# Layer 1 of a four-layer graph network: mark matmuls first, an edge sum in one pass over high and low halves, row one-hots from a distance, their bf16 copy on GpSimd

## The reference, cut to what matters

```python
g_l = (h @ W_l.T).reshape(b, n, H, F)                  # H = 8 heads, F = 16
g_r = (h @ W_r.T).reshape(b, n, H, F)
g_sum = g_r[:, :, None, :, :] + g_l[:, None, :, :, :]  # every pair (i, j)
e = einsum('bijhf,f->bijh', leaky_relu(g_sum, 0.2), w_attn)
e = where(mask == 0, -inf, e * mask)
a = softmax(e, axis=2)
attn_res = einsum('bijh,bjhf->bihf', a, g_r)
out = leaky_relu(attn_res.reshape(b, n, H * F), 0.2)
x = layernorm(x + out)
```

## Time and profile before

| | us |
|---|---|
| median of 3 runs | 1573.96 |
| lowest and highest | 1572.91, 1576.82 |
| the profiled execution | 1573.45 |
| its span in the profile | 1571.7 |

### The profile page before, as it was taken

The page is one execution under the profiler, slowest core; times in us unless marked ns, Lnnn a source line. Parts: engine busy times, 40 slices in busy tenths (PEclk is TensorE's granted clock), DMA queues, the critical chain, the costliest instruction groups (busy, mean ns, idle before and its releaser), DMA issues. The chain is left out here.

```text
span 1571.7 us, 28366 instructions
## 1 busy us (share of the span) xinstructions
PE 1380.7 (88%) x9081; PEld 1163.2 (74%) x9081; DVE 1251.6 (80%) x2450; ACT 1044.8 (66%) x2743; POOL 55.9 (4%) x88
## 2 busy tenths in 40 slices
PE   3666588999999999999999986999999999995764
PEld 2555366688888888888888885888888888884654
DVE  4888478778787878878787644898889989987888
ACT  2565588766666666666666213888888888886554
POOL 1000000000000000000000000010010110100000
PEclk9998699999999999999999997999999999998877
DMA  2220266888887878878888665988787788771122
GB/s 75 68 67 27 112 258 247 320 310 292 299 304 291 308 288 308 306 283 309 299 296 303 236 243 206 349 274 279 271 271 280 267 275 278 268 253 47 45 74 67
DMA packets 137585, 367.61 MB, mean 234 GB/s; under 512 B 12896, under 2 KB 71904, under 8 KB 137440
## 3 DMA queue, kind: packets, MB, share of 16 engines
q1 hardware_dynamic: 137040, 365.81, 65.8%
q10 hardware_dynamic: 400, 0.00, 0.0%
HBM read 231.54 MB, written 134.22 MB: 233 GB/s over the span
## 5 line engine op out<-in xcount | busy, mean ns | idle before, releaser
L874 DVE TENSOR_TENSOR b_wt<-bank,b_aT 128x512 f32<-128x512 f32 (+1 forms) x192 | 109.7, 599 | 95.2 <-PE bank L688 88.1
L647 PE MATMUL wide<-b_vv,put_w 128*128 128x512 f32 (+1 forms) x384 | 170.9, 527 | 12.8 <-DVE b_vv L823 10.8
L1054 PE MATMUL wide<-W2c,c_h 128*128 128x128 f32 x1280 | 173.9, 275 | 0.0
L1054 PEld LDWEIGHTS wide<-W2c,c_h 128*128 128x128 f32 x1280 | 170.4, 193 | 3.3
L664 PE MATMUL bank<-b_wt,b_SITl 128*128 128x136 f32 x1280 | 160.1, 280 | 9.4 <-DVE b_wt L874 9.4
L664 PEld LDWEIGHTS bank<-b_wt,b_SITl 128*128 128x128 f32 x1280 | 156.3, 190 | 16.0 <-DVE b_wt L874 12.0
L823 DVE TENSOR_TENSOR b_vv<-duo,b_vv 128x512 f32<-128x512 f32 (+1 forms) x192 | 113.8, 600 | 51.4 <-ACT b_vv L744 51.4
L688 PE MATMUL bank<-b_grl,b_SJl 128*128 128x128 f32 x1280 | 153.4, 275 | 0.6 <-ACT b_aT L751 0.6
L688 PEld LDWEIGHTS bank<-b_grl,b_SJl 128*128 128x128 f32 x1280 | 148.7, 192 | 2.8 <-issue 2.6
L1184 DVE TENSOR_REDUCE c_var<-c_ysq 128x4 f32<-128x512 f32 (+1 forms) x192 | 113.5, 591 | 43.2 <-ACT c_ysq L1113 43.0
L648 PE MATMUL wide<-b_SI,put_m 128*128 128x512 f32 (+1 forms) x192 | 131.6, 686 | 0.0
(11 more groups left out here) (212 smaller groups left out, 3180.4 us busy)
## 6 DMA issues: line engine op xcount, KB each, us to landing
si_d<-b_SI SPq DMA_DIRECT2D x64, 640.0 KB, 2.9
sj_d<-b_SJ SPq DMA_DIRECT2D x64, 640.0 KB, 4.1
sit_d<-b_SIT SPq DMA_DIRECT2D x64, 640.0 KB, 5.3
b_SJl<-sj_d SPq DMA_DIRECT2D x64, 640.0 KB, 5.8
b_SITl<-sit_d SPq DMA_DIRECT2D x64, 640.0 KB, 5.9
c_SJ<-sj_d SPq DMA_DIRECT2D x64, 640.0 KB, 5.3
c_SI<-si_d SPq DMA_DIRECT2D x64, 640.0 KB, 6.6
c_SIT<-sit_d SPq DMA_DIRECT2D x64, 640.0 KB, 4.2
```

Of the source, the lines that this page charges most:

```text
L647: pe.matmul(out, e.put_w[:, pos, :], vv[:, (pos + k) % 2, 0:width(k)], start=(pos == 0), stop=False)
L874: v.tensor_tensor(wt[:, mb, 4 * k:4 * k + rr, 0:P].rearrange("p r (h f) -> p r h f", h=HEADS), ring[k][:, 0:P * rr].rearrange("p (r h f) - ...
L1054: d = pe.matmul(bY[k][:, a:a + P], h[:, k, a:a + P], e.W2c[:, :], start=False, stop=(j == last))
```

## The change

Four things change, all in layer 1:

- **Sum over halves.** ACT casts `wt` to fp32r into the first 136 columns of `wh` (three instructions, L816 after), DVE writes the rest, `wt` minus that, into the other 136 (three, L929), and PE sums both with 10 fp32r matmuls of 272 columns (L673), for 10 fp32 ones of 136. ACT copies two results out (`ol`, `os`; L776, L777), and DVE adds them once for four graphs (L897).
- **Marks first.** The three mark matmuls of a step stand together ahead of the first score (L659), and no longer one behind each score.
- **Row one-hots from a distance.** ACT takes the absolute distance of each slot number from the middle of a row's range in f32 (L360), and DVE compares it with half the row's length in one `tensor_scalar` (L369), for a `scalar_tensor_tensor` over two tensors.
- **The bf16 copy `SIb`** is made by GpSimd (L377), in a queue of its own.

```diff
 def start_rows(act, e, s, K, pos, late):
-    act.activation(s.after[:, :], e.number1[:, :], ACT.Relu, bias=e.unfirst[:, bass.ds(n, 1)]).then_inc(s.after_ok, 1)
+    act.activation(s.far[:, :], e.number1[:, :], ACT.Abs, bias=e.unmid[:, n:n + 1]).then_inc(s.far_ok, 1)
 def select_rows(v, e, s, K, pos, late):
-    v.scalar_tensor_tensor(s.SI[:, pos % 4, :], e.number1[:, :], e.end[:, bass.ds(n, 1)], s.after[:, :],
-                           ALU.is_le, ALU.min).then_inc(s.si_ok, 1)
+    v.tensor_scalar(s.SI[:, pos % 4, :], s.far[:, :], e.half[:, n:n + 1], None, ALU.is_le).then_inc(s.si_ok, 1)
+def shorten_rows(pool, s, n):
+    pool.wait_ge(s.si_ok, n + 1)
+    if n >= 1:
+        pool.wait_ge(s.s_mm, 3 * n)
+    pool.tensor_copy(s.SIb[:, :], s.SI[:, n % 4, :].bitcast(F32)).then_inc(s.sib_ok, 1)
...
@@ PE
-                        pe.matmul(out, e.put_w[:, pos, :], vv[:, (pos + k) % 2, 0:width(k)], start=(pos == 0), stop=False)
-                        pe.matmul(out, e.put_m[:, pos, :], s.SI[:, pos % 4, chunk(k)], start=False,
+                        pe.matmul(out, e.put_w[:, pos, :], vv[:, (pos + k) % 2, 0:width(k)], start=False,
                                   stop=(pos == R - 1)).then_inc(e_mm, 1)
+                    def mark_rows():
+                        if pos == 0 and n > 0:
+                            pe.wait_ge(es_ok, K)
+                        for k in range(CHUNKS):
+                            pe.matmul(bE[:, chunk(k)], e.put_m[:, pos, :], s.SI[:, pos % 4, chunk(k)], start=(pos == 0), stop=False)
...
-                        pe.wait_ge(w_ok, 3 * o + 3)
-                        pe.wait_ge(wa_ok, o + 1)
+                        pe.wait_ge(wl_ok, 3 * o + 3)
...
-                            d = pe.matmul(ring[1][:, 0:W], SITl[:, ob, j, :], wt[:, ob, j, :],
+                            d = pe.matmul(ring[1][:, 0:2 * W], SITl[:, ob, j, :], wh[:, ob, j, :],
@@ ACT
+                        act.copy(ol[:, (o // Q) % 2, o % Q, :], ring[1][:, W:2 * W])
                         act.copy(os[:, (o // Q) % 2, o % Q, :], ring[1][:, 0:W]).then_inc(os_ok, 1)
...
-                    if N:
-                        shorten_rows(act, s, K, pos + 1, inner or g >= 1)
...
+                    if S:
+                        for k in range(CHUNKS):
+                            js = slice(tiles(k).start, tiles(k).stop)
+                            act.wait_ge(w_ok, 3 * m + k + 1)
+                            act.wait_ge(wa_ok, m + 1)
+                            if m >= 2:
+                                act.wait_ge(o_mm, m - 1)
+                            act.copy(wh[:, mb, js, 0:W], wt[:, mb, js, :]).then_inc(wh_ok, 1)
@@ DVE
+                        f.add(v.tensor_tensor(part, part, ol[:, fours(n) % 2, :, :], ALU.add))
+                        f.wait()
...
+                    if S:
+                        for k in range(CHUNKS):
+                            js = slice(tiles(k).start, tiles(k).stop)
+                            v.wait_ge(wh_ok, 3 * m + k + 1)
+                            v.tensor_tensor(wh[:, mb, js, W:2 * W], wt[:, mb, js, :], wh[:, mb, js, 0:W].bitcast(F32),
+                                            ALU.subtract).then_inc(wl_ok, 1)
```

More of the change, by code:

```diff
@@ L296, in _ @@
                 q.add(v.tensor_copy(e.first[:, :], bank[:, 0:B]))
-                q.add(v.tensor_scalar(e.unfirst[:, :], bank[:, 0:B], -1.0, None, ALU.mult))
                 q.add(v.tensor_reduce(worst[:, 0:1], bank[:, P:P + B], AX.X, ALU.max))
@@ L300, in _ @@
                 q.wait()
-                q.add(v.tensor_tensor(e.end[:, :], e.first[:, :], e.deg[:, 0, :], ALU.add))
+                q.add(v.tensor_scalar(e.half[:, :], e.deg[:, 0, :], 0.5, -0.5, ALU.mult, ALU.add))
+                q.add(v.scalar_tensor_tensor(e.unmid[:, :], e.deg[:, 0, :], 0.5, e.first[:, :], ALU.mult, ALU.add))
                 q.add(v.tensor_scalar(worst[:, 0:1], worst[:, 0:1], float(ECAP), None, ALU.is_gt))
@@ L304, in _ @@
                 q.wait()
+                q.add(v.tensor_scalar(e.unmid[:, :], e.unmid[:, :], -1.0, -0.5, ALU.mult, ALU.add))
                 q.add(v.tensor_tensor(e.general[:, :], worst[:, 0:1], worst[:, 1:2], ALU.max))
@@ L358, in start_rows @@
         act.wait_ge(s.si_ok, n)
-    act.activation(s.after[:, :], e.number1[:, :], ACT.Relu, bias=e.unfirst[:, bass.ds(n, 1)]).then_inc(s.after_ok, 1)
+    act.activation(s.far[:, :], e.number1[:, :], ACT.Abs, bias=e.unmid[:, n:n + 1]).then_inc(s.far_ok, 1)
 def select_rows(v, e, s, K, pos, late):
     n = 8 * K + pos
-    v.wait_ge(s.after_ok, n + 1)
+    v.wait_ge(s.far_ok, n + 1)
     if late:
         v.wait_ge(s.u_mm, 3 * n - 9)
-    v.scalar_tensor_tensor(s.SI[:, pos % 4, :], e.number1[:, :], e.end[:, bass.ds(n, 1)], s.after[:, :],
-                           ALU.is_le, ALU.min).then_inc(s.si_ok, 1)
[L372 to L378, removed]
+    v.tensor_scalar(s.SI[:, pos % 4, :], s.far[:, :], e.half[:, n:n + 1], None, ALU.is_le).then_inc(s.si_ok, 1)
[4 more added lines that the diff above has]
+    pool.tensor_copy(s.SIb[:, :], s.SI[:, n % 4, :].bitcast(F32)).then_inc(s.sib_ok, 1)
 def split_low(v, s, bank, K, pos, late, hi_count):
@@ L466, in layer1_packed @@
         s.C = sb("C", [P, 2, P], F32R)
-        s.after = sb("after", [P, ECAP], BF16)
+        s.far = sb("far", [P, ECAP])
         s.SI = sb("SI", [P, 4, ECAP], F32R)
@@ L489, in layer1_packed @@
         wt = sb("wt", [P, 2, TILES, W])
+        wh = sb("wh", [P, 2, TILES, 2 * W], F32R)
         os = sb("os", [P, 2, Q, W])
+        ol = sb("ol", [P, 2, Q, W])
         rden = sb("rden", [P, Q, HEADS])
@@ L530, in layer1_packed @@
         wa_ok = sem("wa_ok")
+        wh_ok = sem("wh_ok")
+        wl_ok = sem("wl_ok")
         o_mm = sem("o_mm")
@@ L622, in _ @@
                 pool.memset(mark[:, ECAP:ECAP + 1], 0.0).then_inc(pad_ok, 1)
+                for n in range(B):
+                    shorten_rows(pool, s, n)
             @block.tensor
@@ L691, in step @@
                     if A and not T:
-                        if pos == 0 and n > 0:
-                            pe.wait_ge(es_ok, K)
+                        mark_rows()
                         score(0)
@@ L888, in step @@
                     if joined(n):
-                        f = Steps(v, seq_c, 5 * fours(n))
-                        f.n = 3
+                        f = Steps(v, seq_c, 6 * fours(n))
+                        f.n = 4
                         f.wait()
@@ L1900, in adjacency_stack @@
         first = sb("first", [P, B])
-        unfirst = sb("unfirst", [P, B])
-        end = sb("end", [P, B])
+        unmid = sb("unmid", [P, B])
+        half = sb("half", [P, B])
         general = sb("general", [P, 1], I32)
@@ L2072, in adjacency_stack @@
         e.first = first
-        e.unfirst = unfirst
+        e.unmid = unmid
         e.identb = identb
-        e.end = end
+        e.half = half
         e.general = general
```

19 lines of the change are left out of this document (10 added, 9 removed).

## The result

The changed kernel takes 1623.5 us (median of 4 runs, 1619.3 to 1627.0) where the kernel before took 1573.8 beside it: a ratio of 1.030, 95% interval 1.0286 to 1.0321. It is 3% slower. The forecast was 1617, in a range of 1555 to 1648. The total was nearly right by luck, for two of its terms were not right: the overlap's was 21 us too large, the drain's 28 us too small.

What follows compares the result with a forecast made beforehand. PE bounds the overlap, with DVE nearly as full; after the change DVE was followed as the limit. Overlap +26, fill -5 and drain +22 make +43 on 1573.45, about 1617 us; own range 1600 to 1635, over the cases 1555 to 1648.

Steps and rivals of the forecast that it cites:

- the overlap's: Overlapped stretch of layer 1: steps of 12.2 us on average, 0.55 more than before, times 48 steps: +26 us.
- the drain's: Drain of layer 1: steps of 7.0 us on average where they took 5.6, +19 us over 13 steps.
- POOL's hold: DVE in layer 1: POOL's bf16 copy holds up `C`, by 0 to 1.4 us, taken as 0.7 a step.
- Fill: Fill of layer 1: about 0.7 of 8.2 us a step saved, POOL's hold takes 0.35 back; 14 steps: -5 us.
- Casts and subtractions: ACT and DVE: casts 1.4 to 1.5 us, subtractions 1.6; PE gets the sum's input 0.3 us late.
- the rival at 1652: Overlap: POOL holds `C` for its whole 1.6 us copy, 1.35 late; steps average 12.85, +57 us; chance 0.13.
- max(8.3, 7.2 + X) + 2.5: Overlapped step's length in us: third bend at 8.3 by PE or 7.2 + X by DVE, then 2.5 to next step.
- X: Overlap: DVE's extra work ahead of the third bend, such as softmax instructions (1.45 us) and batch work (2.45 in steps 3, 7).
- PE stays the bound: Overlap: waits shrink when DVE runs late and absorb X, steps 10.9 us on average; 1535 us, more likely 1555; chance 0.24.
- Marks: PE: two marks leave the piece from third bend to next step; 0.34 us there in overlap, 0.34 + 0.23 in fill.
- the chain that the prediction names: Drain: casts, subtractions and batch work stand between `wt` and PE's sum; steps 7.0 us for 5.6, +19 us.
- the tail's 3: After the drain's 13 steps: the last graphs' sum and add come 3 us later.

Runs made afterwards that it cites:

- x1: The changed kernel with the bf16 copy SIb back on ACT, in its old place: 1597.2 us, ratio 1.014 to the kernel before.
- x6: The changed kernel, POOL's copy kept, with DVE's scan and `C` moved behind the first two bends: 1604.3 us, ratio 1.019 to the kernel before.
- z1: y1 with the batch work of four graphs spread over two steps: 1541.3 us, ratio 0.9795 to the kernel before.
- x4: The changed kernel without halves, all sums in fp32 from `wt`: 1574.7 us, ratio 1.0004 to the kernel before.
- z2: x4 with each mark matmul behind its score again, as before the change: 1575.5 us, ratio 1.0009 to the kernel before.
- x3: The changed kernel with 8 to 18 bf16 matmuls on constants in PE's waiting time of every drain step: 1598.5 us, ratio 1.0154 to the kernel before.
- z3: The changed kernel with DVE's batch work behind the subtractions in the drain, not ahead: 1598.1 us, ratio 1.0158 to the kernel before.
- x2: The changed kernel with graphs 48 to 63 summed in fp32 from `wt`, without casts and subtractions: 1576.0 us, ratio 1.0015 to the kernel before.
- y1: The changed kernel with x1 and x2 together: 1548.8 us, ratio 0.983 to the kernel before.

## Why the prediction was right, and where not

*Direction and size.* Right: slower by 3.0% where 2.7% was forecast. In the overlap the forecast's own mechanism, POOL's hold with DVE as the bound, is what the traces show, but it costs that stretch 5 us and not 26. The size of the total is luck: against the forecast the overlap came out 21 us shorter and the drain's 13 steps 28 us longer. Half of the real loss, the clock, was priced at nothing.

*The sum on PE.* 1.26 us for ten matmuls, 1.2 expected.

*Fill.* As expected: its steps went from 8.05 to 7.66 us, and the hold takes 0.30 of each (x1) where 0.35 was taken.

*Row one-hots.* 0.88 us by the group's mean, 0.80 to the next start; 0.75 expected.

*Casts and subtractions.* Three subtractions 1.6 us, as expected. DVE waits about 0.4 us for the first cast behind a light step (the last row of the first timeline above), where 0.5 was expected in every step.

*POOL's hold.* It works in that direction too. 0.79 us on `C`, 0.7 taken; x1 shows 0.48 of it in the length of an overlapped step and 0.30 in a fill step. The rule of the Trainium skill that was weighed ("SBUF — State Buffer", "Who interferes with whom": whoever starts first has the pair for the whole instruction) agrees with the trace for `C`: it ends 0.15 after the end of the copy. So the mechanism was that of the rival at 1652, a hold for the whole copy, and not the forecast's something in between; only the size was near the forecast's 0.7, because the copy takes 1.25 us undisturbed (x6), not 1.6, and 1.38 here. The rival shared the forecast's two large errors besides.

*The overlapped stretch: the term that was too large.* The step "max(8.3, 7.2 + X) + 2.5" gave 12.2 us; 11.76 was measured, and without the hold 11.27 (x1) for 11.65. X is not what was wrong: from step 3 to step 7 of eight it falls by 1.5 us and the step by 1.37 (13.28 to 11.91, from `lo` to `lo`). What was wrong is the constant, in two ways. First, the forecast let the subtractions wait for the casts in every step. The wait is there only behind a light step (X of 0 to 2.05, in 0, 2, 4 and 6). Behind a heavy one (X of 2.45 or more) DVE comes late to `lo`, and the casts are ready. So it is there at the start of steps 1, 3, 5 and 7 and gone in 0, 2, 4 and 6. Timeline of DVE, changed kernel, the start of step 3 and then of step 6:

```profile
631.12 0.42 DVE L386 TENSOR_TENSOR b_lo<-duo,b_hi 128x256 fp32r<-128x256 f32 x1 [0.43 <-ACT b_grs L806]
631.95 1.71 DVE L929 TENSOR_TENSOR b_wh<-b_wt,b_wh 128x544 fp32r<-128x544 f32 x3 [0.41 <-ACT b_wh L816]
```

```profile
761.45 0.41 DVE L386 TENSOR_TENSOR b_lo<-duo,b_hi 128x256 fp32r<-128x256 f32 x1
761.78 1.70 DVE L929 TENSOR_TENSOR b_wh<-b_wt,b_wh 128x544 fp32r<-128x544 f32 x3
```

The subtractions start 0.83 after `lo` in the one and 0.33 in the other. Second, the rest of DVE's path was counted too long. Steps 1, 3, 5 and 7 keep the wait and are still shorter than forecast: 12.1, 13.3, 12.1 and 11.9 for 12.5, 13.65, 12.5 and 12.15. One piece of it is the way from the third bend to the next step's first gather on PE, 2.34 us in step 3 (642.53 to 644.87) for 2.5. Step 4, without the wait, takes 10.97 for 11.75, while in step 2 (10.92 for 11.2) a wait of 0.43 ahead of the next `lo`, the one in the first row above, takes most of the gain back. In all that is 0.45 a step, or 21 us. (By its own formula the forecast's steps 3 and 6 come to 13.6 and 11.75, not 13.65 and 12.0, which is 2 of these 21.)

The rival "PE stays the bound" had named the wait that shrinks when DVE runs late, and z1 shows the other half of it: work goes free of charge into a step where DVE still waits. It was wrong on the result, for in the heavy steps DVE has no wait left, and there X counts in full (z1, step 3: about 1.1 us less work, 1.15 less time).

*Marks.* That two marks leave the loop was priced as a gain on PE. In the overlap it is a loss of 0.12 us a step when PE is the bound (x4, z2). It is a gain of about 0.5 in a fill step, where PE waited anyway.

*The drain: the term that was too small.* At the full clock the 13 steps would have cost 20.8 us more; 19 were expected, by the chain that the prediction names, and the tail's 3 became 4.7. The other 26 are the clock (x3). This is the step of the prediction that failed: it saw PE's gap of up to 4.9 us (4.76 measured), noted that no row of before had its like, and priced nothing. A bound could have been worked out from its own terms: PE has a gather of 2.24 and a sum of 1.2 us in each drain step, an estimate of 45 us in 13 steps, and at the lower level of the clock these could take up to 45 us more. z3 agrees, but moves the chain and the clock together and can't price the clock by itself.

## What to carry to other kernels

Work that makes one engine's matmuls cheaper and two others' queues longer pays only where the first is the bound; look at fill, overlap and drain apart, since an edit that is nearly neutral in one can cost over 40 us in another (overlap and drain of the changed kernel: +5.0 and +46.9), and apply it only where it pays (x2, y1). What halves are worth in y1 was not measured alone; x4, without them, has steps of 11.65 in the overlap where y1 has 11.28. Where engines wait for each other in a fixed order, a heavy step is not paid back by a light one: moving a part of the batch work from a full step to the one before it, in which DVE still waited, gave 7.5 us with the same work (1548.8 to 1541.3, z1). Before a copy goes to GpSimd, look at what DVE runs beside it: an instruction with two SBUF inputs waits for its end, one that reads PSUM and SBUF does not.

## What was not expected of the hardware

- With PE idle for 2.1 to 4.8 us in each step of 6.6 to 11.5, the granted clock was 0.71 on average over 120 us; with gaps of 2.3 us it was 0.85 (z3), and with the gaps filled by matmuls on constants down to 0.6 to 0.9 us, but for the first, it was 1.00 (x3). Useless matmuls in PE's waiting time made the kernel 25 us faster.
- Three fp32r matmuls of marks in one piece cost PE 0.67 us, and the scores without them 0.86, 0.86 and 0.50; the same six in turns cost 0.16 less, 0.12 of which shows in the step (x4, z2). Why is left open.
- POOL's copy of 1,280 elements from f32 to bf16 took 1.25 us undisturbed and 1.38 where a DVE scan with two SBUF inputs ran for the first 0.33 us of it (599.83 to 600.16). `C`, which came later, was held until the copy's end. Why the scan cost the copy only 0.13 is left open.
